# A conv chain with a state-space scan on one Trainium2 core: which steps' state pairs GpSimd adds and which TensorE sums itself

## What is computed

```
def step(hst, xs):
    d_t, B_t, C_t, u_t = xs
    dA = jnp.exp(d_t[:, :, None] * A)
    hst = hst * dA + (d_t * u_t)[:, :, None] * B_t[:, None, :]
    y_t = jnp.einsum('bdn,bn->bd', hst, C_t)
    return (hst, y_t)
```

## Time and profile before

| | us |
|---|---|
| three timed runs | 6263.67 to 6267.61, median 6267.37 |
| the profiled execution's own time | 6269.85 |
| its span, first to last instruction | 6268.0 |
| PE busy | 5262.4 (84%) |
| DVE busy | 5166.1 (82%) |
| POOL busy | 3934.6 (63%) |
| ACT busy | 3677.1 (59%) |
| mean granted TensorE clock | 0.953 |

### The profile page before, as it was taken

The page is one execution under the profiler, slowest core; times in us unless marked ns, Lnnn a source line. Parts: engine busy times, 40 slices in busy tenths (PEclk is TensorE's granted clock), DMA queues, the critical chain, the costliest instruction groups (busy, mean ns, idle before and its releaser), DMA issues.

```text
span 6268.0 us, 78256 instructions
## 1 busy us (share of the span) xinstructions
PE 5262.4 (84%) x18611; PEld 2958.7 (47%) x18611; DVE 5166.1 (82%) x6330; ACT 3677.1 (59%) x6045; POOL 3934.6 (63%) x2702
## 2 busy tenths in 40 slices
PE   6688888888888888888888888888888888888871
PEld 6244444444544444454444444444444444444441
DVE  4788888888888888888888888888888888888843
ACT  2556656665665666566566556556656655665633
POOL 0776666666666666666666666666666666666620
PEclk8799999999999999999999999999999999999996
DMA  3555555455555555555555555555555555455526
GB/s 119 215 211 202 191 197 199 182 203 194 191 200 196 192 190 202 198 187 202 191 190 199 196 198 190 195 195 187 202 197 197 194 201 195 183 204 194 196 112 271
DMA packets 199097, 1215.89 MB, mean 194 GB/s; under 512 B 27880, under 2 KB 28656, under 8 KB 67696
## 3 DMA queue, kind: packets, MB, share of 16 engines
q1 hardware_dynamic: 194416, 1196.26, 52.5%
q10 hardware_dynamic: 4352, 16.78, 0.7%
HBM read 1158.43 MB, written 54.53 MB: 194 GB/s over the span
## 4 chain that ended last, share of the span: by engine, by line
PE 53%; DVE 17%; issue 15%; ACT 11%; DMA 1%; DVEq 1%; ACTq 1%; POOL 0%; SPq 0%; POOLq 0%
PE psE L828 16%; PE psT L828 12%; PE psA L828 11%; PE psY L828 8%; DVE hs L485 5%; DVE psD L481 5%; PE psT L1003 5%; ACT p L735 4%; DVE nm L517 3%; ACT da L694 2%; ACT pt L704 2%; DVE xn L461 1%; ACT delta L678 1%; ACT sp_e L676 1%; PE psD L828 1%
## 5 line engine op out<-in xcount | busy, mean ns | idle before, releaser
L296 POOL TENSOR_TENSOR pa<-hs,rows_all 128x1024 f32<-128x1024 f32 x1024 | 2411.0, 2355 | 1841.9 <-DVE hs L485 1836.3
L694 ACT ACTIVATE da<-delta,neg_a 128x512 f32<-128x512 f32 x2048 | 1372.5, 720 | 221.0 <-DVE hs L485 177.5
L481 DVE TENSOR_TENSOR psD<-rows_all,psU 128x512 f32<-128x512 f32 x2048 | 1414.8, 691 | 104.9 <-DVE psU L474 42.6
L485 DVE TENSOR_TENSOR_SCAN hs<-da,hlast,psD 128x512 f32<-128x512 f32 x1024 | 1310.9, 1280 | 37.5 <-ACT da L694 1.2
L485 DVE TENSOR_TENSOR_SCAN hs<-da,psD 128x512 f32<-128x512 f32 x1024 | 1249.0, 1220 | 35.9 <-ACT da L694 0.7
L828 PE MATMUL psY<-pa,ident 128*128 128x512 f32 x2304 | 1203.9, 619 | 64.3 <-POOL pa L303 46.7
L303 POOL TENSOR_TENSOR pa<-pa 128x512 f32<-128x512 f32 x896 | 1147.1, 1280 | 35.1
L735 ACT ACTIVATE p<-psE,nm 128x1024 f32<-128x1024 f32 x512 | 572.9, 1119 | 692.7 <-DVE nm L517 688.3
L828 PE MATMUL psA<-pt,va 128*128 128x256 f32 x4096 | 932.5, 381 | 31.2 <-DVE x L537 26.6
L828 PEld LDWEIGHTS psA<-pt,va 128*128 128x128 f32 x4096 | 775.3, 190 | 259.0 <-issue 156.2
L517 DVE TENSOR_REDUCE nm<-psE 128x1 f32<-128x1024 f32 x512 | 620.5, 1212 | 245.8 <-PE psE L828 239.9
(11 more groups left out here) (181 smaller groups left out, 4780.9 us busy)
## 6 DMA issues: line engine op xcount, KB each, us to landing
rows_all<-bc_scratch SPq DMA_DIRECT2D x1024, 1024.0 KB, 4.7
xin<-x SPq DMA_DIRECT2D x40, 512.0 KB, 7.1
xres<-x SPq DMA_DIRECT2D x64, 256.0 KB, 6.1
x_scratch<-x SPq DMA_DIRECT2D x32, 512.0 KB, 6.5
f_scratch<-fa SPq DMA_DIRECT2D x32, 512.0 KB, 6.6
xres<-x SPq DMA_DIRECT2D x8, 512.0 KB, 3.3
x1g<-x SPq DMA_DIRECT2D x8, 512.0 KB, 3.3
fa<-x SPq DMA_DIRECT2D x8, 512.0 KB, 3.3
```

The lines of the kernel that those rows point to most:

```text
L296: pool.tensor_tensor(pa[:, k % PROD, :, :], hs[:, sl, :, :], rows_all[:, slot, 2:4, :], ALU.mult).then_inc(S["prod"], 1)
L481: dve.tensor_tensor(psD[:, :], rows_all[:, slot, j, :], psU[:, :], ALU.mult).then_inc(S["dbu_ok"], 1)
L485: dve.tensor_tensor_scan(hs[:, sl, j, :], da[:, sl, j, :], psD[:, :], hlast[:, h, n_:n_ + 1] if ch else 0.0, ALU.mult, ALU.add).then_inc(S ...
L694: act.activation(da[:, k % 2, j, :], delta[:, h, cols(ch)], ACT.Exp, scale=neg_a[:, h, 2 * q + j:2 * q + j + 1]).then_inc(S["da_ok"], 1)
```

## The change

GpSimd adds the pair in nine of the 16 steps of a half (0, 1, 2, 5, 6, 10, 11, 12, 13) and no longer in steps 3, 4, 7, 8, 9. For these five and for 14 and 15 as before, TensorE sums both products.

```
-ADDED = [r for r in range(16) if r not in (14, 15)]
+ADDED = [0, 1, 2, 5, 6, 10, 11, 12, 13]
```

## The result

The changed kernel took 6421.93 us, the median of four runs from 6414.49 to 6426.08, beside 6267.49 before. The ratio is 1.0241 with a 95% interval from 1.0221 to 1.026: slower by 2.4%, 154 us. The forecast was 6381, 114 us slower, with a range from 6328 to 6428. The profiled execution took 6414.49 us and its span is 6412.7 us, against 6268.0 before.

A forecast was written before the change was run, and what follows sets the result against it. A closed chain through PE, DVE and ACT sets the period. Exposed matmuls cost 129 us, the clock returns 15: +114 us on the execution's own 6269.85 gives 6384, or 6381 against the median; range 6328 to 6428.

The forecast's parts named there:

- The chain and the places: Closed chain through PE, DVE and ACT; added matmuls cost only where PE does not wait: 4.16 us per image.
- Step 5: Ahead of inner0, the 0.86 us matmul fits into PE's wait for xn (2.01 and 2.81 us): cost 0.
- Step 6: Between inner1 and project_values, 0.08 us is covered by the wait for xc and 0.78 exposed per half.
- Steps 9 to 11: Three matmuls ahead of the energy of tile 2 outlast the wait for dts, moving it 1.30 us per half.
- GpSimd's relief: Taking 320 additions, 410 us, off POOL is worth 0, since POOL is nearly always out of the chain.
- The interference: Rival: without POOL's addition, DVE's xn in step 5 gets 0.4 us shorter, 25 us less, 6356; chance 0.05.
- the clock: PE falls to 1.2 GHz after some waits; less idle time gives back 0.5 us per image, 15 us.
- dearer: Rival: the clock falls in more images (1.5) and its 0.5 is not given back, 6443; chance 0.08.
- step 9: Ahead of weigh0: DVE's attended waits for rb, a copy of PE's psA, so DVE moves by the whole 0.86 us.
- The rival of the clock: The second half's inner0 runs at full clock, 3.0 us less per image, 6287; in every second image 6334; chance 0.10.

The follow-up runs named there:

- the kernel with it alone: GpSimd gives up the five additions, TensorE sums only the first product of those pairs, matmuls as in the kernel before: 6278.62 us, 1.0004 of it.
- step 3 alone: Against the kernel before, GpSimd gives up only the pair of step 3, summed by TensorE in step 5: 6238.17 us, ratio 0.9935.
- the filled wait: Changed kernel with step 4's sum moved behind the energy of step 7, into PE's wait for va: 6285.52 us, 1.0015 of the kernel before.
- The kernel with all pairs added: Against the kernel before, GpSimd adds the pairs in all 16 steps, 14 and 15 too: 6251.21 us, ratio 0.9957.
- the one that fills the waits: Step 3 given up, 14 added by GpSimd, step 4's sum and skip0 moved into the wait for va: 6096.47 us, 0.9713 of the kernel before.

## Why the prediction was right, and where it was off

- *The chain and the places.* Right. Step 5 cost 0: in the second half `xn` is awaited for 2.80 us as before. Step 6 was put at 0.78 and stands in the table with 0.60 and 0.66. In the first half, at full clock, it is 0.67 (11.52 to 12.19 us from `inner0` to that `energy`, medians): `project_values` starts the full 0.78 later, but goes out in 1.95 us in place of 2.05 when it does not wait for `xc`. DVE's wait went from 0.63 to 1.30 (forecast about 1.4). In the second half the clock's falls are mixed in. Steps 9 to 11 were put at 1.30 and measured 1.40. The sum was put at 4.16 us per image, and the rows of the table that hold new matmuls give 4.07.
- *GpSimd's relief.* Right at 0: the kernel with it alone gives 1.0004.
- *The interference.* Right to leave it out: `xn` stayed at 1047 ns.
- *The step that failed: the clock.* I gave 0.5 us per image back, 15 us, on the thought that the half-clock time falls with PE's idle time. Idle time fell by 17%, from 23.5 to 19.4 us, and nothing came back: the time at 1.2 GHz rose from 10.6 to 12.2 us per image. The stretches with unchanged work grew by about 0.4 us per image up to the image's end; a new one at 1.2 GHz stands behind the `energy` of tile 2, where two waits used to be, and only the turn of the image got faster. I forecast 3.66 us per image net and the period grew by 4.5, which is 26 us of the 30 between the 6384 forecast for the execution's own time and its 6414.49. The other 10 us up to the median: the profiled execution lies 7.4 below its runs' median, where the one of before lay 2.5 above. The measured 6422 lies nearer to the rival "dearer" (6443) than to the forecast (6381), and what that rival names, more time at 1.2 GHz, did happen, at about half its size: 1.6 us more per image is at most 0.8 us of work, against its 1.5. That the result fell inside the range, 6 us from its end, owes something to luck.
- *A step that was right by luck: step 9.* "DVE moves by the whole 0.86 too" is wrong. Alone it moves by 0.33, since ACT's queue covers 0.53. The sum came out because in the whole change PE itself, not `dts`, releases the `energy`. I had read the idle time before `attended` (1.26 us, ended by `rb`) and not the one before `rb`, which was none.
- *Two slips that moved nothing.* The price of "dearer" is 4.16 + 1.5 = 5.66 us per image, which gives 6443; "6.2" adds the 0.5 that 4.16, with nothing given back, already holds. And `dts` is no fair measure for an undisturbed `xn`: it is a copy of 8 partitions out of PSUM. The `xn` without POOL beside it happens to take the same 0.69 us.
- *The rival of the clock.* It was given 0.10 and a price for the whole change. It is real for step 3 alone (41 us faster, 7.8 us at 1.2 GHz) and for the filled wait, and absent in the change.

## What to carry to other kernels

A matmul costs what its place leaves exposed, and an engine's wait is one cover for all that is put ahead of it: sum the additions between two waits first, and subtract the wait once. For each wait on the way ask also what the releasing engine was doing before, since a queue there is a second cover. Work given to a busy engine belongs right into its longest wait; here that also kept it at full clock, and the same matmuls cost 2.4% in one order and 0.15% in another.

## What the runs showed of the hardware that was not expected

- The clock's part is as large as the work's. The same 896 conv records took from 419.5 us to 496.9 us over 28 images, with nothing changed but other work in the image. The kernel with all pairs added has the fewest matmuls and a mean clock of 0.944; the one that fills the waits has 0.965 and is 155 us faster. In every trace the granted clock has two levels only, 2.4 and 1.2 GHz; the time at the lower one went from 4.8 to 17.6 us per image. What decides it was not settled.
- Costs of about one microsecond per image can vanish. The kernels that give up 4, 7, or 8 and 9 alone have 1.6, 0.7 and 0.9 us per image more by places, yet ended within 0.2% of before. The time at 1.2 GHz moved the other way in two of them, 8.9 and 9.4 us per image against 10.6. Why it should is open.
- A filled wait of 1.08 us for `va` leaves the records behind it at 2.4 GHz (598 ns), one of 2.80 us often does not (742 ns).
- Beside a product of GpSimd, which reads SBUF, DVE's `xn` with two SBUF inputs takes 0.91 to 1.11 us, alone 0.69; GpSimd's additions, gone or not, change nothing of it (1047 ns).
